# Returning the routed rows by indirect DMA through DRAM instead of by selection matrices on TensorE

## The chip, the core and the metric

One core of a Trainium2 chip runs the whole kernel in one launch. The metric is the device time of one execution in microseconds (us); the median of three runs of the kernel before is 292.20 us (292.16 to 292.22).

## What is computed

One transformer layer for x of 2 batches x 512 rows x 256 columns, float32: attention with 16 heads of width 128 over one shared latent k, a layernorm, then a network that only half of the rows pass (the 256 of 512 with the highest router score), and a second layernorm over all rows.

```python
x = _layernorm(x + attention(x, W_lat, b_lat, W_d, b_d, W_proj, b_proj))
scores = jnp.einsum('bsd,d->bs', x, router_weight) + router_bias[0]
top_scores, indices = jax.lax.top_k(scores, K)              # K = 256 of 512
weights = jax.nn.sigmoid(top_scores)
selected = jnp.take_along_axis(x, indices[:, :, None], axis=1)
h = jax.nn.gelu(jnp.einsum('bkd,df->bkf', selected, w1) + b1)      # 256 -> 1024
processed = jnp.einsum('bkf,fd->bkd', h, w2) + b2                  # 1024 -> 256
out = flat.at[flat_idx].add((processed * weights[:, :, None]).reshape(b * K, d))
x = _layernorm(out.reshape(b, s, d))
```

A row that isn't picked keeps its value, and its second layernorm depends on nothing but itself.

## The kernel before

Rows lie on 128 partitions: 4 tiles (TILES) per batch, `x1[:, b * 4 + j, :]` being 128 rows of 256. Every float32 product is three matmuls on two float32r words, high and low (`product`, L364 to L369): ScalarE writes a high word (`..._hi`), VectorE or POOL subtracts it to get the low one (`..._lo`).

The engines' programs are written by hand, each in order, with semaphores between them. Attention runs in periods, one per head and batch: units 0 to 31, and in period p TensorE does scores(p), turn(p-1), queries(p+1), project(p-2), values(p-1). `periods` (L262) walks through them; 3 to 12 are a loop, the rest is written out. Batch 0 ends its attention in period 17, so its layernorm, router, ranks and choice are put in pieces into periods 18 to 29 (names AT_OUT to AT_SELECT_T2, L278 to L280), on VectorE through `middle_piece` (L952) and `last_piece` (L980). On POOL each period splits W_d, W_proj and, in 13 to 28, a part of the network's weights.

The routing: `router_dots` (L1055) takes the dot with the router's weights on rows not yet normalised; `router_scores` scales them by the inverse deviation, which POOL computes as a power (`inverse_deviation`, L1290). TensorE turns the scores to a row (`turn_scores`, L521), `compare` (L1074) counts who beats whom, `rank_cols` (L527) sums on TensorE, and `ranks` (L1096) gives each row's rank. From the rank, `select` (L1104) builds a 0/1 matrix `sel` (a row's rank against 0 to 255), and TensorE gathers the picked rows, turned, into PSUM by 16 matmuls (`gather`, L545). ScalarE and VectorE take `xs_hi` and `xs_lo` from it. `rank_rows` (L536) turns the ranks to a row and `select_turned` (L1111) builds the opposite matrix `selT`.

The network: `hidden` (L563) makes 8 chunks of 6 matmuls, ScalarE the gelu and high word, POOL (batch 0) or VectorE (batch 1) the low word; `net_out` (L591) makes 24 matmuls for each of two groups of 128 picked rows; `start_net` (L580) puts b2 into PSUM beforehand. `net_high` (L817) and `net_low` (L1127) split the result, `scatter` (L602) spreads it over the 512 rows by 16 matmuls with `selT`, `add_up` (L1132) adds it to x1 times the weight and sums, and layernorm and stores follow (STORES, L354, from SP). For batch 1 the last variance goes through ScalarE's Square (L838), `last_variance` (L1179), POOL's power (L1320) and `last_apply` (L1185).

The order after attention: batch 0's gather stands in period 32 (two halves around the turns), hidden(0, 0..1) in period 33 ahead of the last projection; then TensorE runs hidden(0), start_net, net_out(0) with turn_scores(1) and rank_cols(1) between, rank_rows(1), gather(1), scatter(0), hidden(1), net_out(1), scatter(1). VectorE and ScalarE keep the matching order; VectorE does batch 0's add_up between the low words of hidden(1).

Of the kernel before, what the change touches and what calls it, by code (L numbers as in the profile page):

```python
# [28 lines left out]
F32 = mybir.dt.float32  # L29
F32R = mybir.dt.float32r  # L30
BF16 = mybir.dt.bfloat16
# [3 lines left out]
P = 128  # L35
# [21 lines left out]
def mk_layer_kernel(nc, x, W_lat, b_lat, W_d, b_d, W_proj, b_proj, router_w, router_b,  # L57
                    w1, b1, w2, b2, out):
    with ExitStack() as top:
# [7 lines left out]
        x1 = sb("x1", [P, BATCH * TILES, DIM])  # L67
# [14 lines left out]
        iota_col = sb("iota_col", [P, RCH])  # L82
# [13 lines left out]
        st = sb("st", [P, BATCH * 2, TILES, 6])  # L96
        mv = sb("mv", [P, BATCH * 2, TILES, 2])
        ve = sb("ve", [P, BATCH * 2, TILES])
        rstd = sb("rstd", [P, BATCH * 2, TILES])

        z_sum, minus_mean, squares = (sb(n, [P, TILES]) for n in ("z_sum", "minus_mean", "squares"))
# [8 lines left out]
        rank_row = sb("rank_row", [P, SEQ])  # L110
        rank = sb("rank", [P, TILES], F32R)
        half_tanh = sb("half_tanh", [P, BATCH, TILES])
        ones_row = sb("ones_row", [1, P], F32R)
        b2_hi, b2_lo = sb("b2_hi", [1, DIM], F32R), sb("b2_lo", [1, DIM], F32R)
        weight = sb("weight", [P, BATCH, TILES])
        x1_hi = sb("x1_hi", [P, BATCH * TILES, DIM], F32R)
        x1_lo = sb("x1_lo", [P, BATCH * TILES, DIM], F32R)
        sel = sb("sel", [P, BATCH * TILES, KEEP], F32R)
        selT = sb("selT", [P, BATCH, RCH, SEQ], F32R)
# [8 lines left out]
        def sems(name):  # L128
# [7 lines left out]
        b2_hi_done, b2_split = sem("b2_hi_done"), sem("b2_split")  # L136
# [25 lines left out]
        compared, rank_row_ready, rank_ready, rank_row_done, rank_done = (  # L162
            sems(n) for n in ("compared", "rank_row_ready", "rank_ready", "rank_row_done", "rank_done"))
        sel_done, selT_done, tanh_done, weight_done = (
            sems(n) for n in ("sel_done", "selT_done", "tanh_done", "weight_done"))
        x1_hi_done, x1_split = sems("x1_hi_done"), sems("x1_split")
# [3 lines left out]
        net_ready, net_hi_done, net_split = (  # L170
            sems(n) for n in ("net_ready", "net_hi_done", "net_split"))
        minus_mean_done, squares_done, last_var_done = (
            sem(n) for n in ("minus_mean_done", "squares_done", "last_var_done"))
        scattered, sum_done, stored = sems("scattered"), sems("sum_done"), sems("stored")
# [45 lines left out]
        net_hi = sb("net_hi", [P, BATCH, RCH, DIM], F32R)  # L220
        net_lo = sb("net_lo", [P, BATCH, RCH, DIM], F32R)
# [40 lines left out]
        def periods(eng, body):  # L262
# [11 lines left out]
        CONSTS = 7  # L274
# [5 lines left out]
         AT_SELECT, AT_SELECT_T, AT_SELECT_T2) = range(AT_OUT + 1, AT_OUT + 13)  # L280
# [7 lines left out]
        hidden_banks = [ps_s10, ps_s3, ps_s2, ps_y]  # L288

        def hidden_bank(f):  # L290
            return hidden_banks[f % len(hidden_banks)][:, 0:KEEP]

        def net_bank(b, r):
            return ps_out[:, 2 * r + b, :]

        def scatter_bank(b, j):


            if b:
                return (ps_t0, ps_t1, ps_s2, ps_s3)[j][:, 0:DIM]  # L300
            return (ps_t0, ps_t1)[j // 2][:, (j % 2) * DIM:(j % 2 + 1) * DIM]

        def chosen_bank(c):
            return (ps_s3, ps_s2)[c][:, 0:KEEP]

# [6 lines left out]
        def _(sp):  # L312
# [39 lines left out]

            periods(sp, period)
            STORES = [(0, 0, 2), (0, 2, 4), (1, 0, 2), (1, 2, 3), (1, 3, 4)]  # L354
            for b, j0, j1 in STORES:
                sp.wait_ge(ln_done[b], TILES + j1)
                sp.dma_start(out[b, j0 * P:j1 * P].rearrange("(j p) d -> p j d", p=P),
                             x1[:, b * TILES + j0:b * TILES + j1, :]).then_inc(stored[b], 16)
            for b in range(BATCH):
                sp.wait_ge(stored[b], 16 * len([st for st in STORES if st[0] == b]))  # L360

        @block.tensor
        def _(pe):
# [86 lines left out]
            def turn(at, n):  # L450
# [7 lines left out]
                if n == 1 and at.fixed - 1 in (AT_TURN, AT_SELECT, AT_RANK):  # L458

                    pe.wait_ge({AT_TURN: score_row_done, AT_SELECT: rank_row_done, AT_RANK: rank_done}[at.fixed - 1][0], 1)  # L460
# [75 lines left out]
            def rank_rows(b, dst):  # L536

                pe.wait_ge(rank_done[b], 1)
                for j in range(TILES):
                    last = pe.transpose(dst[:, j * P:(j + 1) * P].bitcast(F32R), rank[:, j:j + 1].to_broadcast([P, P]),  # L540
                                        ident_r[:, :])
                last.then_inc(rank_row_ready[b], 1)


            def gather(b, tiles=range(TILES)):  # L545

                pe.wait_ge(x1_split[b], 2)
                pe.wait_ge(negmax_done, 4 * UNITS)
                if b:
                    pe.wait_ge(xs_split[0], CH)  # L550
                    pe.wait_ge(gelu_done[0], FCH)
                for j in tiles:
                    pe.wait_ge(sel_done[b], j + 1)
                    for c in range(CH):
                        t, cs = b * TILES + j, slice(c * P, (c + 1) * P)
# [790 lines left out]
```

## Time and profile before

| | us |
|---|---|
| median of three runs | 292.20 |
| the profiled execution | 292.16 |
| its span in the trace | 290.40 |

| engine | busy us | share of the span |
|---|---|---|
| TensorE (PE) | 280.5 | 97% |
| VectorE (DVE) | 224.0 | 77% |
| ScalarE (ACT) | 211.4 | 73% |
| POOL | 144.9 | 50% |

The span is the time from the first to the last recorded event of the core; 1.76 us of the execution lie outside it. A busy share is an average over the whole kernel: what bounds a stretch has to be read from that stretch. In the traces L12 is line 12 of the kernel, and start times count from the span's start. The next instruction of an engine may start before the end of the one before it, since matmuls and others are pipelined: of a group of n, the time from start to start counts. No DMA of this kernel is issued from POOL.

### The profile page before, as it was taken

What the parts mean: (1) busy time and instruction counts of PE and PEld (TensorE: products, weight loads), DVE (VectorE), ACT (ScalarE), POOL (GpSimd) and SP (SyncE); (2) the same over time, 40 slices, a digit from 0 to 9 for tenths busy, and PEclk for the clock granted to TensorE, in tenths of its full rate; (3) what the DMA queues carried; (4) which work ended last, traced back from release to release, by engine and by line L of the source; (5) the groups of instructions that cost most, each with busy time, mean ns of one, the idle gap of its engine ahead of it and who ended that gap; (6) DMA issues with size and microseconds to landing.
All of it is one profiled execution on the core that took longest, in us unless ns stands there. A gap on an engine that the chain in (4) does not pass through costs nothing.

```text
span 290.4 us, 6306 instructions
## 1 busy us (share of the span) xinstructions
PE 280.5 (97%) x1942; PEld 255.1 (88%) x1942; DVE 224.0 (77%) x699; ACT 211.4 (73%) x582; POOL 144.9 (50%) x204
## 2 busy tenths in 40 slices
PE   6998999999999999999999999999999999999991
PEld 3777999999999999999999999999999999999991
DVE  2688777777777777777888788999888877498685
ACT  3588777777777777777777777777798777663632
POOL 3647643444343448655556756656557612184013
PEclk9999999999999999999999999999999999999997
DMA  6583111111111111111101111111110000000004
GB/s 190 119 283 98 39 38 36 36 36 36 36 36 36 36 37 38 36 35 40 34 26 42 32 35 36 40 36 36 40 37 20 19 21 0 2 1 0 2 9 136
DMA packets 17738, 13.42 MB, mean 46 GB/s; under 512 B 1433, under 2 KB 17458, under 8 KB 17714
## 3 DMA queue, kind: packets, MB, share of 16 engines
q1 hardware_dynamic: 17714, 13.13, 15.4%
q8 instruction: 12, 0.20, 0.3%
q14 instruction: 12, 0.10, 0.1%
HBM read 12.07 MB, written 1.05 MB: 45 GB/s over the span
## 4 chain that ended last, share of the span: by engine, by line
PE 88%; DVE 6%; ACT 2%; issue 1%; SPq 1%; DMA 1%; POOL 1%; POOLq 0%; DVEq 0%; ACTq 0%
PE bank L367 18%; PE bank L369 17%; PE bank L368 17%; PE bank L468 8%; PE ps_out L367 7%; PE ps_out L369 6%; PE ps_out L368 6%; PE bank L518 2%; PE bank L446 2%; DMA bias_rows<-in_L_ffn_b 1%; DVE x L1052 1%; PE bank L556 1%; DVE sel L1060 1%; PE bank L558 1%; DVE beats L1087 1%
## 5 line engine op out<-in xcount | busy, mean ns | idle before, releaser
L725 ACT ACTIVATE probs<-probs,negmax 128x512 f32<-128x512 f32 (+3 forms) x128 | 72.6, 574 | 7.1 <-DVE negmax L891 5.7
L1213 POOL TENSOR_TENSOR wd_hi<-wd_raw,zero 128x256 fp32r<-128x256 f32 x32 | 24.7, 772 | 89.4 <-DVE probs L948 83.8
L732 ACT CAST pT_hi<-bank 128x512 fp32r<-128x512 f32 (+2 forms) x96 | 43.5, 488 | 28.7 <-PE bank L468 28.7
L891 DVE CUSTOM_DVE_ANT_0 probs<-bank,mask_row 128x512 f32<-128x512 f32 (+3 forms) x128 | 59.2, 482 | 0.6 <-PE bank L369 0.6
L898 DVE TENSOR_TENSOR pT_lo<-bank,pT_hi 128x512 fp32r<-128x512 f32 (+2 forms) x96 | 53.0, 553 | 6.2 <-ACT pT_hi L732 5.9
L468 PEld LDWEIGHTS bank<-ident_r,prob_words 128*128 128x128 f32 x320 | 34.4, 141 | 5.3 <-issue 0.2
L367 PE MATMUL ps_out<-wp_hi,yT_hi 128*128 128x256 f32 x128 | 38.4, 300 | 0.1
L367 PE MATMUL bank<-kT_hi,qT_hi 128*128 128x512 f32 (+2 forms) x96 | 37.3, 389 | 0.2 <-DVE qT_lo L845 0.2
L908 DVE TENSOR_TENSOR yT_lo<-bank,yT_hi 128x512 fp32r<-128x512 f32 x32 | 22.1, 691 | 18.5 <-PE bank L369 13.3
L369 PE MATMUL ps_out<-wp_hi,yT_lo 128*128 128x256 f32 x128 | 36.2, 283 | 0.0
L368 PE MATMUL ps_out<-wp_lo,yT_hi 128*128 128x256 f32 x128 | 36.1, 282 | 0.0
L468 PE MATMUL bank<-ident_r,prob_words 128*128 128x128 f32 x320 | 35.0, 240 | 0.0
L367 PE MATMUL bank<-pT_hi,k_hi 128*128 128x512 f32 (+2 forms) x96 | 32.9, 342 | 0.9 <-DVE pT_lo L898 0.9
L369 PE MATMUL bank<-kT_hi,qT_lo 128*128 128x512 f32 (+2 forms) x96 | 32.6, 340 | 0.0
L368 PE MATMUL bank<-pT_lo,k_hi 128*128 128x512 f32 (+2 forms) x96 | 32.4, 337 | 0.0
L368 PE MATMUL bank<-kT_lo,qT_hi 128*128 128x512 f32 (+2 forms) x96 | 32.3, 337 | 0.0
L369 PE MATMUL bank<-pT_hi,k_lo 128*128 128x512 f32 (+2 forms) x96 | 32.2, 335 | 0.0
L1213 POOL TENSOR_TENSOR wp_hi<-wp_raw,zero 128x256 fp32r<-128x256 f32 x32 | 23.6, 738 | 13.7 <-DVE probs L948 13.7
L948 DVE TENSOR_SCALAR probs<-probs,rinv 128x384 f32<-128x384 f32 (+2 forms) x96 | 28.3, 351 | 1.1
L764 ACT ACTIVATE probs<-probs,rinv 128x512 f32<-128x512 f32 x32 | 23.2, 724 | 8.2 <-DVE rinv L942 8.2
L845 DVE SCALAR_TENSOR_TENSOR qT_lo<-bank,bias_cols,qT_hi 128x384 fp32r<-128x384 f32 x32 | 19.7, 616 | 12.1 <-ACT qT_hi L695 11.7
L367 PE MATMUL bank<-xT_hi,wd_hi 128*128 128x512 f32 x64 | 27.8, 434 | 0.0
(150 smaller groups left out, 744.0 us busy)
## 6 DMA issues: line engine op xcount, KB each, us to landing
wd_raw<-in_L_attn_W_d SPq DMA_DIRECT2D x32, 128.0 KB, 2.2
wp_raw<-in_L_attn_W_proj SPq DMA_DIRECT2D x32, 128.0 KB, 2.1
wf_raw<-in_L_ffn_w SPq DMA_DIRECT2D x2, 1024.0 KB, 6.5
x_nat<-in_L_attn_x SPq DMA_DIRECT2D x4, 256.0 KB, 3.0
out<-x SPq DMA_DIRECT2D x3, 256.0 KB, 2.2
out<-x SPq DMA_DIRECT2D x2, 128.0 KB, 2.0
wlat_raw<-in_L_attn_W_lat SPq DMA_DIRECT2D x1, 128.0 KB, 3.5
bproj_all<-in_L_attn_b_proj SPq DMA_DIRECT2D x1, 128.0 KB, 3.7
```

The lines of the kernel that those rows point to most:

```text
L367: pe.matmul(dst, lh, rh, start=first, stop=False, skip_group_check=check)
L368: pe.matmul(dst, lh, rl, start=False, stop=False, skip_group_check=check)
L369: return pe.matmul(dst, ll, rh, start=False, stop=last, skip_group_check=check)
L468: last = pe.transpose(dst[:, a:a + P].bitcast(F32R), prob_words[s][:, P_OFF[j] + i * P:P_OFF[j] + (i + 1) * P], ident_r[:, :])
L725: act.activation(p_tile(s, j), p_tile(s, j), ACT.Exp, bias=negmax[:, s, j:j + 1], scale=-1.0, accum_out=sums[:, s, j:j + 1]).then_inc(exp_ ...
L732: act.copy(pT_hi[:, turns[n][3]], turns[n][2]).then_inc(pt_hi_done, 1)
L764: act.mul(p_tile(at.place(0), 3), p_tile(at.place(0), 3), rinv[:, at.place(0), 3:4]).then_inc(norm_act, 1)
L891: dve.tensor_tensor_reduce(p_tile(s, j), score_bank[j], mask_row[:, (TILES - 1 - j) * P:], -SCALE, -MASKED, ALU.add, ALU.min, accum_out=ne ...
L898: dve.tensor_tensor(pT_lo[:, dst], src, pT_hi[:, dst].bitcast(F32), ALU.subtract).then_inc(pt_lo_done, 1)
L908: dve.tensor_tensor(yT_lo[:, :], ps_y[:, :], yT_hi[:, :].bitcast(F32), ALU.subtract).then_inc(y_lo_done, 1)
L948: dve.tensor_scalar(p_tile(s, j), p_tile(s, j), rinv[:, s, j:j + 1], None, ALU.mult).then_inc(norm_dve, 1)
L1213: pool.tensor_tensor(hi, src, nothing, ALU.add).then_inc(hi_done, 1)
```

## The change

Picked rows no longer go through selection matrices, but for batch 1's gather.

Batch 0: each row of x1 gets two words more, its gate (sigmoid of the score) and its number. After the ranks POOL issues four indirect DMAs (`push`), each writing 128 rows to DRAM at their rank (`ranked`); SP loads the first 256 back (`picked`, `load_picked`, period 29); TensorE turns them by four transposes (`turn_picked`, period 31) into the xs of the network. Batch 1 keeps `sel` and `gather`, is pushed and loaded too, but only for what follows.

All 512 rows of a batch are normalised without a network's share into `z_all` and stored. The network's output of a batch (`net_bank`) is added to `z`, which POOL begins as b2 times gate plus picked row (`begin_z`); two tiles of `z` are normalised and `put_back` writes them by two indirect DMAs per batch onto the stored output. So `selT`, `rank_rows`, `start_net`, `net_high`, `net_low` and both scatters are gone. hidden(0) starts a period earlier, with chunks 0 to 2 in period 32 and 3 and 4 in 33, and its banks are three.

```diff
+            def load_picked(b):
+                sp.wait_ge(pushed[b], 16 * TILES)
+                sp.dma_start(picked[:, b].bitcast(F32), ranked[b][0:KEEP, :].rearrange("(r p) d -> p r d", p=P)
+                             ).then_inc(picked_in[b], 16)
...
+                if at.fixed == AT_REST_2:
+                    load_picked(0)
...
+            store_all(0)
+            load_picked(1)
+            store_all(1)
...
+            def turn_picked():
+                pe.wait_ge(picked_in[0], 16)
+                pe.wait_ge(negmax_done, (UNITS - 1) * 4 + 1)
+                for c in range(CH):
+                    for r in range(RCH):
+                        last = pe.transpose(ps_s3[:, c * KEEP + r * P:c * KEEP + (r + 1) * P].bitcast(F32R),
+                                            picked[:, 0, r, c * P:(c + 1) * P], ident_r[:, :])
+                last.then_inc(gathered[0], 1)
...
-            hidden(0, range(2, 6))
-            start_net()
-            hidden(0, range(6, FCH))
-            net_out(0, 0, range(0, 4))
+            hidden(0, range(5, FCH))
+            net_out(0, 0)
             turn_scores(1, ps_t0)
-            net_out(0, 0, range(4, FCH))
-            net_out(0, 1, range(0, 4))
+            net_out(0, 1, range(0, 6))
             rank_cols(1, ps_t1)
-            net_out(0, 1, range(4, FCH))
-            rank_rows(1, ps_t0)
-            gather(1)
-            scatter(0)
+            net_out(0, 1, range(6, FCH))
+            gather()
             hidden(1, range(FCH))
             for r in range(RCH):
                 net_out(1, r)
-            scatter(1)
```

VectorE after the periods (routing of batch 1, low words, the two tails):

```diff
-            layernorm_apply(1, 0, range(TILES))
+            layernorm_apply(1, 0, (0, 1))
             compare(1, range(TILES))
             losses(1)
-            net_low(0, 0)
+            layernorm_apply(1, 0, (2, 3))
             ranks(1, ps_t1)
-            select(1, range(TILES))
-            net_low(0, 1)
-            chosen_low(1)
-            for q in range(RCH):
-                select_turned(1, q)
-            weights(1)
+            select((0, 1))
+            dve.wait_ge(x1_hi_done, 2)
+            dve.tensor_tensor(x1_lo[:, 2:TILES, :], x1[:, TILES + 2:2 * TILES, :], x1_hi[:, 2:TILES, :].bitcast(F32),
+                              ALU.subtract).then_inc(x1_split[1], 1)
+            select((2, 3))
+            rank_numbers()
+            gates(1)
+            chosen_low()
...
+            for f in range(FCH):
+                hidden_low(f)
+                if f < TILES:
+                    layernorm_stats(1, 1, (f,))
+                    aggregate(1, 1, (f,))
+                elif f == TILES:
+                    variance(1, 1, 0)
+                    variance(1, 1, 1)
+                else:
+                    layernorm_apply(1, 1, (f - TILES - 1,))
+            layernorm_apply(1, 1, (3,))
+            for r in range(RCH):
+                add_up(0, r)
+            layernorm_stats(0, 2, range(RCH))
+            aggregate(0, 2, range(RCH))
+            variance(0, 2, 0)
+            add_up(1, 0)
+            layernorm_apply(0, 2, range(RCH))
...
+            last_variance(0)
             last_apply(0)
-            last_variance((3,))
-            for j in range(1, TILES):
-                last_apply(j)
+            add_up(1, 1)
+            last_variance(1)
+            last_apply(1)
```

POOL:

```diff
+            def push(b):
+                pool.wait_ge((rank_no_done if b else rank_done)[b], 1)
+                pool.wait_ge(gate_done[b], 1)
+                pool.wait_ge(consts, CONSTS)
+                for j in range(TILES):
+                    pool.wait_ge(ln_done[b], j + 1)
+                    pool.indirect_dma_start(ranked[b], bass.IndirectOffsetOnAxis(ap=rank_no[:, b, j:j + 1], axis=0),
+                                            x1_row[:, b * TILES + j, :], None).then_inc(pushed[b], 16)
+
+            def begin_z(b):
+                pool.wait_ge(picked_in[b], 16)
+                pool.wait_ge(rows_in, 64)
+                for r in range(RCH):
+                    pool.tensor_scalar(z[:, b, r, :], b2_all[:, :], gate(b, r), None, ALU.mult).then_inc(b2_gated[b], 1)
+                    pool.wait_ge(b2_gated[b], r + 1)
+                    pool.tensor_tensor(z[:, b, r, :], z[:, b, r, :], picked_words(b, r, 0, DIM),
+                                       ALU.add).then_inc(z_begun[b], 1)
+
+            def put_back(b, r):
+                pool.wait_ge(stored[b], 32)
+                pool.wait_ge(ln_done[b], 2 * TILES + r + 1)
+                pool.indirect_dma_start(out.rearrange("b s d -> (b s) d"),
+                                        bass.IndirectOffsetOnAxis(ap=picked[:, b, r, ROW_NO:ROW_NO + 1].bitcast(U32), axis=0),
+                                        z[:, b, r, :], None).then_inc(routed[b], 16)
...
             for f in range(FCH):
-                if f in (2, 3):
-                    inverse_deviation(1, 0, f - 2)
+                if f in (6, 7):
+                    inverse_deviation(1, 0, f - 6)
                 hidden_low(f)
+            x1_low(0)
+            push(1)
             for half in range(2):
-                x1_low(1, half)
-            for half in range(2):
-                inverse_deviation(0, 1, half)
...
+                inverse_deviation(1, 1, half)
+            begin_z(1)
+            inverse_deviation(0, 2, 0)
+            for r in range(RCH):
+                put_back(0, r)
+            for r in range(RCH):
+                pool.wait_ge(last_var_done, r + 1)
+                pool.tensor_tensor(rstd[:, 2 * BATCH + 1, r:r + 1], ve[:, 2 * BATCH + 1, r:r + 1],
+                                   minus_half[:, r:r + 1], ALU.pow).then_inc(rstd_done[1], 1)
+                put_back(1, r)
```

push(0) stands at the end of POOL's period 27 (AT_PUSH). `layernorm_stats(b, 1, ...)`, `aggregate`, `variance` and `layernorm_apply(b, 1, ...)` now serve the rows without a network's share, those with 2 the picked ones; batch 0's stand in periods 27 to 31.

## Rows read from the trace of the kernel before

**Rows 1.** Stretches of all engines: us, busy (x instructions) of PE, PEld, DVE, ACT, POOL; clock; DMA

```profile
171.12:178.47 7.35, 7.35 (x54) 6.74 (x52) 6.48 (x23) 5.73 (x17) 4.54 (x6) 1.00 0.13 36
208.63:216.32 7.69, 7.69 (x60) 7.08 (x58) 6.16 (x21) 5.90 (x17) 4.40 (x6) 1.00 0.12 35
254.07:264.79 10.72, 10.32 (x80) 9.53 (x80) 10.48 (x35) 6.18 (x16) 8.62 (x11) 1.00 0.00 1
264.79:270.72 5.93, 5.93 (x58) 5.93 (x59) 4.17 (x13) 1.53 (x4) 0.67 (x1) 1.00 0.01 3
270.72:276.47 5.75, 5.75 (x50) 5.75 (x49) 3.43 (x15) 4.59 (x13) 0.00 (x0) 1.00 0.00 0
276.47:282.33 5.86, 5.86 (x52) 5.86 (x51) 4.75 (x19) 1.65 (x5) 1.38 (x2) 1.00 0.00 0
282.33:290.40 8.07, 2.12 (x17) 1.74 (x15) 4.52 (x19) 2.44 (x9) 2.19 (x4) 0.81 0.39 130
```

**Rows 2.** The chain that ended last, from 235 us: start us, us, what

```profile
253.39 0.70 DVE x L1014
...
262.85 1.90 DVE beats L1087 x8
...
285.34 1.71 POOL rstd L1320 x3
...
287.57 0.41 DVE x L1188
```

**Rows 3.** TensorE's groups from 238 us: count | busy us, mean ns | idle

```profile
L556 PE MATMUL bank<-sel,x_hi 128*128 128x256 f32 x16 | 4.2, 297 | 0.0
L617 PE MATMUL bank<-net_hi,selT 128*128 128x256 f32 x16 | 4.0, 287 | 0.0
```

**Rows 4.** POOL in order of time

```profile
216.68 1.29 POOL L1300 TENSOR_TENSOR x_lo<-x,x_hi 128x512 fp32r<-128x512 f32 x1 [3.41 <-ACT x_hi L775]
...
257.29 0.80 POOL L1295 TENSOR_TENSOR rstd<-ve,minus_half 128x2 f32<-128x2 f32 x1 [0.17 <-DVE ve L1042]
258.06 3.99 POOL L1306 TENSOR_TENSOR hid_lo<-hid,hid_hi 128x256 fp32r<-128x256 f32 x5
...
279.46 0.69 POOL L1295 TENSOR_TENSOR rstd<-ve,minus_half 128x2 f32<-128x2 f32 x1 [14.00 <-DVE ve L1039]
```

**Rows 5.** VectorE in order of time: start us, us, line, operation [idle before]

```profile
259.27 0.57 DVE L1068 TENSOR_TENSOR dots_scaled<-dots,rstd 128x4 f32<-128x4 f32 x1
...
260.53 2.32 DVE L1052 TENSOR_SCALAR x<-x,mv,rstd 128x256 f32<-128x256 f32 x4
...
264.77 0.70 DVE L1094 TENSOR_TENSOR lost<-behind,won 128x4 f32<-128x4 f32 x1
...
265.91 1.14 DVE L1108 TENSOR_SCALAR sel<-iota_row,rank 128x256 fp32r<-128x256 f32 x4
...
273.15 0.43 DVE L1168 TENSOR_TENSOR hid_lo<-hid,hid_hi 128x256 fp32r<-128x256 f32 x1 [2.32 <-ACT hid_hi L799]
...
278.15 0.74 DVE L1026 BATCH_NORM_STATS2 st<-x 128x6 f32<-128x256 f32 x2
...
281.26 1.39 DVE L1052 TENSOR_SCALAR x<-x,mv,rstd 128x256 f32<-128x256 f32 x4 [0.54 <-POOL rstd L1295]
...
283.89 0.48 DVE L1139 SCALAR_TENSOR_TENSOR x<-bank,weight,x 128x256 f32<-128x256 f32 x1 [0.69 <-PE bank L618]
```

**Rows 6.** ScalarE in order of time

```profile
268.79 0.67 ACT L815 ACTIVATE xs_hi<-bank 128x256 fp32r<-128x256 f32 x2 [1.16 <-PE bank L558]
...
284.42 0.51 ACT L838 ACTIVATE squared<-x,z_sum 128x256 f32<-128x256 f32 x1 [1.68 <-DVE x L1139]
```

**Rows 7.** SP's stores (L357): issue in ns, min/median/max, and landing

```profile
L357 SPq DMA_DIRECT2D out<-x x5: 373/394/402, 282.0 to 288.0; - x5
...
DMA to landing us min/median/max: 1.9/2.2/2.3
```

**Rows 8.** POOL's groups over the whole span: the longest operation

```profile
L1286 POOL TENSOR_TENSOR x<-x_nat,bproj_all 128x1024 f32<-128x1024 f32 x2 | 4.8, 2389 | 0.0
```

More of the change, by code:

```diff
@@ L628, in period @@
                 if at.fixed == UNITS:
-                    gather(0, range(0, 2))
+                    hidden(0, range(0, 2))
                 if at.live(-1):
@@ L644, in period @@
                 else:
+                    if at.fixed == AT_PICKED:
+                        turn_picked()
                     if at.fixed == UNITS:
-                        gather(0, range(2, TILES))
+                        hidden(0, range(2, 3))
                     if at.fixed == UNITS + 1:
-                        hidden(0, range(0, 2))
+                        hidden(0, range(3, 5))
                     if at.live(-2):
@@ L972, in middle_piece @@
                     layernorm_apply(0, 0, (2,))
-                if at.fixed == AT_SELECT:
-                    select(0, (0,))
-                if at.fixed == AT_SELECT_T:
-                    select(0, (3,))
-                if at.fixed == AT_SELECT_T2:
-                    select_turned(0, 1)
+                if at.fixed == AT_PUSH:
+                    layernorm_stats(0, 1, (0,))
+                if at.fixed == AT_REST:
+                    layernorm_stats(0, 1, (2,))
+                if at.fixed == AT_REST_2:
+                    aggregate(0, 1, range(TILES))
+                    variance(0, 1, 0)
+                    variance(0, 1, 1)
+                if at.fixed == AT_REST_3:
+                    layernorm_apply(0, 1, (0,))
             def last_piece(at):
@@ L1111, in select_turned, with select @@
-            def select_turned(b, q):
-                dve.wait_ge(rank_row_done[b], 1)
-                dve.tensor_scalar(selT[:, b, q, :], rank_row[:, :], iota_col[:, q:q + 1], None,
-                                  ALU.is_equal).then_inc(selT_done[b], 1)
-            def weights(b):
+                dst = rank[:, :] if b else rank_no[:, 0, :]
+                dve.tensor_tensor(dst, src[:, 0:TILES], lost[:, b, :], ALU.add).then_inc(rank_done[b], 1)
+            def select(tiles):
+                dve.wait_ge(rank_done[1], 1)
+                for j in tiles:
+                    dve.tensor_scalar(sel[:, j, :], iota_row[:, :], rank[:, j:j + 1], None,
+                                      ALU.is_equal).then_inc(sel_done, 1)
@@ L1169, in _ @@
                                   ALU.subtract).then_inc(hid_split[1], 1)
+            for f in range(FCH):
+                hidden_low(f)
                 if f < TILES:
-                    add_up(0, f)
-            for half in range(2):
-                layernorm_stats(0, 1, (2 * half, 2 * half + 1))
-                aggregate(0, 1, (2 * half, 2 * half + 1))
-                variance(0, 1, half)
-            net_low(1, 0)
-            layernorm_apply(0, 1, range(TILES))
-            net_low(1, 1)
@@ L1277, in period @@
                         inverse_deviation(0, 0, half)
-                if at.fixed in (AT_SELECT, AT_SELECT_T):
-                    x1_low(0, at.fixed - AT_SELECT)
+                if at.fixed == AT_PUSH:
+                    push(0)
+                if at.fixed == AT_REST_3:
+                    for half in range(2):
+                        inverse_deviation(0, 1, half)
+                if at.fixed == AT_PICKED:
+                    begin_z(0)
             def start_x1(b):
```

367 lines of the change are left out of this document (154 added, 213 removed).

## Prediction

> **What bounds the kernel now.** I read four views in this order: the stretches of the last 40 us, the chain that ended last, each engine's order of time in that stretch, and the DMA issues. The stretches [rows 1] show TensorE busy without a gap in an attention period (7.35 of 7.35 us) and again from 264.79 to 282.33. Between them, 254.07 to 264.79, VectorE is busy 10.48 of 10.72 us while TensorE fills in with batch 0's network: there the chain runs through VectorE, from the last projection's sum at 253.39 to the comparisons that end at 264.75 [rows 2]. From 282.33 to the end it is a relay: last scatter, sums, variance, the power on POOL (1.71 us for three), the last normalisation, a store [rows 2]. So three things set the end: VectorE's routing chain of batch 1, then TensorE from the gather on, then the relay.
>
> The profiled run took 292.16 us with a span of 290.40, so 1.76 us lie outside the span; the median of the runs is 292.20. I sum against the span.
>
> **Part 1, inside attention.** Period 27 (with the four rank transposes and the wait for their row) is 7.69 us against 7.35 [rows 1]: removing them gives back 0.34. `turn_picked` puts four transposes into period 31, at 0.06 to 0.12 us each (+0.3); behind them ScalarE takes xs_hi in one pass of 512 and VectorE its low word, ahead of `turned(2)`, and TensorE's `values` waits for that (+0.3). The batch 0 gather goes (its 16 matmuls are half of the gathers', of which [rows 3] has the x1_hi half), but the same place takes three more hidden chunks (18 matmuls) ahead of the last projection. 48 matmuls take 5.75 us [rows 1], so one is 0.12: -1.9 and +2.2. Net: the last projection ends at 254.1 as before, bounds -0.6 and +0.8.
>
> The four pushes of batch 0 stand on POOL behind the splits of period 27. Queued behind them are the next weight splits, which are needed a whole period later; before, the low word of x1 (1.29 us [rows 4]) stood in the same place and TensorE lost nothing by it. Pushes of up to about 7 us together are hidden, so I cost them at nothing; SP's wait for them holds up only the loads of W_proj, a period early. The norm of all rows of batch 0 (stats, variance, apply) takes the place of select and select_turned on VectorE, about as many microseconds: nothing.
>
> **Part 2, routing of batch 1.** The chain on VectorE keeps its shape but only two of the four applications stand before the comparison. Before, the applications start at 260.53 and the four take 2.32 us beside a working POOL, 1.39 us alone [rows 5]. After:
> start 260.8 (the two powers on POOL now stand behind six and seven low words of 0.80 us each [rows 4], so the second ends near 259.6 where it ended at 258.1, and VectorE wants it at 259.27 [rows 4, 5]: +0.3); two applications 0.7, 261.5; wait for the turned scores 0.1; compare 1.90 [rows 2], 263.5; loss, between 0.2 and the 0.70 of [rows 5], 0.3, 263.8; two applications 0.7, 264.5; rank 0.15; two selects 0.57 (half of 1.14 [rows 5]), 265.2; low word of x1, now on VectorE, 0.70 (the size of the sum in [rows 2]), 265.9; two selects 0.57, 266.5; last matmuls of the gather 0.7, 267.2; xs_hi 0.35 (half of 0.67 [rows 6]) and its low word 0.45, 268.0.
> So hidden(1) starts at 268.0, not at 270.72: **-2.7 us**. The scatter of batch 0 (16 matmuls, half of L617's 16 [rows 3] and their partners with net_lo: 1.9 us) and the second set of rank transposes no longer stand on TensorE, and the scatter no longer covers the wait for xs. TensorE has 66 network matmuls (7.9 us) and 0.8 us of turns to put into 13 us, so it is not the bound here. Bounds for this part -3.3 and -1.8.
>
> **Part 3, the network of batch 1.** 5.75 + 5.86 us [rows 1] as before, to 279.6. VectorE's first low word comes 2.43 us after hidden(1) starts (273.15 [rows 5] against 270.72), so at 270.45. Then it does a low word (0.34), stats (0.37) and an aggregate per chunk, 0.92 us, where ScalarE delivers one each 0.72: 274.15 after four; low word and two variances, 274.8. The applications of batch 1 wait for powers (0.69 [rows 4], 275.6) with the last low words queued behind them on VectorE, and TensorE's net_out waits for those: +0.7, so TensorE ends near 280.3 against 282.33. Net of parts 1 to 3: **-2.0 us**.
>
> **Part 4, the relay.** Before, it took 8.07 us [rows 1]. After, there is no scatter(1), no net_hi and net_lo, and only two tiles of sums. But POOL now issues four indirect stores, and it issues put_back(0,0) and put_back(0,1) ahead of batch 1's first power; VectorE has last_apply(0), which waits for that power, ahead of add_up(1,1); so the two stores of batch 0 stand on the path. The unknown is D, the time POOL is held by one indirect DMA of 128 rows. The trace of before has none. Nearest rows: SP's issue of a store, 0.39 us [rows 7], as the low end; POOL's passes of 0.69 (a power) and 1.29 us (512 elements) [rows 4]; its pass over 1024 elements, 2.39 us [rows 8], as the high end. I take D = 1.0, between the two short POOL rows, since 128 addresses are work in software like theirs. Landing after it: 2.2 less 0.4 from issue [rows 7], 1.8, of which some runs beside the generation: 1.6.
> Applications and low words after 275.6: 2.1 us, with 0.5 for POOL's `begin_z(1)` beside them ([rows 5]: 2.32 against 1.39), 278.2; two add_ups 0.8 [rows 5], stats 0.74, aggregate 0.3, variance 0.2, 280.2; power 0.77, 281.0; apply, 281.4; put_back twice, 0.1 + 0.3 (the second application held off by POOL) + 2D, 283.8; power 0.7, 284.5; last_apply(0), 284.9; add_up(1,1) 0.48, 285.35; Square 0.51 and its read-out 0.2 [rows 6], 286.1; variance 0.2, 286.3; power 0.77, 287.05; apply 0.45, 287.5; put_back(1,1) 0.1 + D, 288.6; landing 1.6, 290.2; 0.1 to the end of the span. **Span 290.3, run 292.1.** What the network gains (-2.0) the relay gives back (+1.9). Each 0.1 us of D is worth 0.3 us.
>
> What the profile shows of POOL and VectorE together is that they hold each other up: the same four applications, 2.32 against 1.39 us [rows 5]. The Trainium skill (SBUF — State Buffer, "SBUF: two separate sides", the box on DVE blocking DMA) says the same lock stops POOL from writing descriptors while VectorE runs such an operation, and has a POOL-issued DMA at about 620 ns alone. By 0.62 for D the sum would be 291.0; the row has the lock for computing operations, and no row has it for descriptors.
>
> **Rivals.**
> B, the stores are cheap: D near 0.5, like SP's issue. Then 3 x 0.5 us less and the second application hardly held: span 288.6, **run 290.4**. For it: 128 rows are little data, and SP needs 0.39 [rows 7]. Against it: POOL takes 0.69 us even for an operation on two elements per lane [rows 4]. The Trainium skill (DMA: Bandwidth & Descriptors, "Anatomy of one DMA") calls the generation small and puts the 2 us into completion, which speaks for B; no run shown here has a DMA from POOL.
> C, POOL becomes the bound: D above 1.25. Then put_back(1,0) too delays the last power, and pushes and `load_picked(1)` (4D and two landings after 266.8) reach into `begin_z(1)`. At D = 1.8: +2.4, +0.55 (put_back(1,0)), +0.35 (held application), +0.5 (begin_z late): span 294.1, **run 295.9**. It decides from D = 1.25 on; slower by the measurable starts at 292.8.
> D, the early half fails: batch 0's picked rows come late to period 31, or TensorE's clock falls. It waits some 4 us in pieces between 254 and 268, where before it waited 0.4; the clock granted is 1.00 in all stretches but the last, where it is 0.81 with TensorE mostly idle [rows 1]. A clock halved for hidden(1) would add some 3 us or more: **run 297**.
>
> **How the numbers follow.** Forecast A (D from 0.8 to 1.25, run 291.2 to 293.1): 0.38. B 0.27, C 0.30, D 0.05. The likeliest case gives 292.1, its own range 291.2 to 293.1. A measurement of this kernel tells 0.2%, 0.6 us, from no change. Faster (below 291.6): B and 0.11 of A, 0.38. Same: 0.20. Slower: 0.07 of A, C and D, 0.42. The range runs from B with somewhat less contention, 289.6, to C at D = 1.8, 296.0.
>
> **What would show it.** Part 1: batch 0's period 31 longer by 0.3 to 0.6 us and the last projection ending at 253.5 to 254.9. Part 2: hidden(1) starting near 268.0. Part 3: net_out(1,1) ending near 280.3, with a wait on hid_lo of batch 1. Part 4: the power of batch 1's first tile right behind put_back(0,1), add_up(1,1) waiting behind last_apply(0) for over 3 us, and from the end of TensorE to the end of the span about 10 us. Wrong if POOL is idle before the last powers, or if the relay follows TensorE directly.

## The result and the profile after

The changed kernel takes 295.03 us (median of four runs, 294.94 to 295.28) against 292.19 us of the kernel before beside it: ratio 1.0098, 95% interval 1.0083 to 1.0113, so 1.0% slower. The profiled execution took 294.99 us with a span of 293.3; 1.7 us lie outside. I had forecast 292.1 us; the range of 289.6 to 296.0 holds the time, the likeliest case (291.2 to 293.1) doesn't. Of the three directions I had given slower the largest chance, 0.42, but the sum itself stood at no change.

The stretches of the kernel after, with the columns of [rows 1]:

```profile
core 0: us, PE busy (x) PEld busy (x) DVE busy (x) ACT busy (x) POOL busy (x), PEclk, DMA share, GB/s
208.72:216.06 7.34, 7.34 (x57) 6.73 (x54) 5.91 (x20) 5.56 (x16) 6.29 (x8) 1.00 0.18 55
238.09:244.90 6.81, 6.64 (x52) 6.02 (x50) 5.60 (x18) 5.20 (x16) 4.77 (x6) 1.00 0.13 41
254.60:268.30 13.70, 11.61 (x97) 10.56 (x96) 11.87 (x44) 4.49 (x12) 7.17 (x9) 1.00 0.00 0
268.30:275.20 6.90, 6.90 (x58) 6.90 (x59) 4.06 (x16) 4.78 (x14) 3.01 (x4) 1.00 0.26 82
275.20:281.23 6.03, 5.13 (x40) 4.68 (x39) 5.35 (x20) 0.97 (x3) 5.13 (x7) 1.00 0.39 127
281.23:293.30 12.07, 0.15 (x2) 0.00 (x0) 2.30 (x10) 1.20 (x4) 5.70 (x7) 0.63 0.13 43
```

The period of 7.69 us of [rows 1] is 7.34. The network of batch 1 starts at 268.30 instead of 270.72 (2.42 earlier), TensorE's last matmul for the network ends at 281.39 instead of 282.33 (0.94 earlier), and from there to the end of the span it is 11.9 us instead of 8.07 (the last stretch above begins 0.16 before that matmul's end). In these 12 us TensorE, VectorE and ScalarE are nearly idle; POOL is busy 5.70. What it does there, POOL in order of time (start us, us, line, operation, idle before and what ended it):

```profile
280.94 0.72 POOL L1276 TENSOR_TENSOR rstd<-ve,minus_half 128x2 f32<-128x2 f32 x1 [0.52 <-DVE ve L1020]
282.95 1.07 POOL L1310 DMA_INDIRECT out<-z,picked  x1 [1.29 <-DVE z L1034]
284.32 0.96 POOL L1310 DMA_INDIRECT out<-z,picked  x1 [0.30 <-issue]
285.31 0.58 POOL L1335 TENSOR_TENSOR rstd<-ve,minus_half 128x1 f32<-128x1 f32 x1
287.13 1.04 POOL L1310 DMA_INDIRECT out<-z,picked  x1 [1.24 <-DVE z L1175]
288.19 0.58 POOL L1335 TENSOR_TENSOR rstd<-ve,minus_half 128x1 f32<-128x1 f32 x1
290.01 1.04 POOL L1310 DMA_INDIRECT out<-z,picked  x1 [1.24 <-DVE z L1175]
```

And VectorE beside it, which waits for those powers and has `add_up(1,1)` behind the first of them:

```profile
281.70 0.74 DVE L1034 TENSOR_SCALAR z<-z,mv,rstd 128x256 f32<-128x256 f32 x2 [0.50 <-POOL rstd L1276]
...
285.92 0.41 DVE L1175 TENSOR_SCALAR z<-z,minus_mean,rstd 128x256 f32<-128x256 f32 x1 [3.36 <-POOL rstd L1335]
286.25 0.48 DVE L1112 SCALAR_TENSOR_TENSOR z<-bank,picked,z 128x256 f32<-128x256 f32 x1
...
287.40 0.15 DVE L1166 TENSOR_SCALAR ve<-squares 128x1 f32<-128x1 f32 x1 [0.67 <-ACT squared L805]
...
288.81 0.41 DVE L1175 TENSOR_SCALAR z<-z,minus_mean,rstd 128x256 f32<-128x256 f32 x1 [1.19 <-POOL rstd L1335]
```

Two things are to be read here. A passing power holds POOL for 0.58 us and an indirect store for 0.96 to 1.07 us, one beside the other in one queue: the power at 285.31 starts when the second store ends. And a store whose data has just come starts late: VectorE's pass of 285.92 ends at 286.33, the store starts at 287.13, 0.80 later (0.79 for the last one, 0.83 for the first), while one that was already released starts 0.30 behind the store before it. The powers have no such delay: the variance of 287.40 is there at 287.55 and only the store keeps POOL until 288.17; at 280.94 the power starts 0.14 behind its variance (280.63 and 0.17).

The last store starts at 290.01 and the span ends at 293.3, 3.3 us on. It lands 2.5 us after its start, at 292.5, which is 1.4 us behind the end of POOL's hold (291.05) and 0.8 us before the end of the span. The chain's last pieces, and the row on the landing of the four stores, counted from each one's start:

```profile
286.39 0.74 issue
287.13 1.04 POOL out L1310
...
289.27 0.50 issue
289.78 1.27 POOLq L60
```

```profile
DMA to landing us min/median/max: 2.4/2.5/2.5
```

### The profile page after: what moved, and what is told of

The parts are those of the page before. It is cut to its first block, busy times and chain, and to the rows that moved or that the text cites. A ratio compares the mean times of both kernels' runs of the same rounds, so it can differ in the third digit from the quotient of the medians.

```text
span 293.3 us, 6209 instructions
## 1 busy us (share of the span) xinstructions
PE 274.9 (94%) x1886; PEld 248.8 (85%) x1886; DVE 221.8 (76%) x698; ACT 206.9 (71%) x569; POOL 159.0 (54%) x219
## 3 DMA queue, kind: packets, MB, share of 16 engines
HBM read 12.60 MB, written 2.63 MB: 52 GB/s over the span
## 4 chain that ended last, share of the span: by engine, by line
PE 82%; DVE 6%; POOL 3%; ACT 3%; issue 2%; SPq 1%; DMA 1%; POOLq 0%; DVEq 0%; ACTq 0%
PE bank L384 18%; PE bank L386 17%; PE bank L385 17%; PE bank L485 8%; PE ps_out L384 6%; PE ps_out L386 5%; PE ps_out L385 5%; PE bank L535 2%; PE bank L463 2%; POOL out L1310 1%; POOL hid_lo L1317 1%; POOL rstd L1276 1%; DMA bias_rows<-in_L_ffn_b 1%; DVE beats L1069 1%; DVE z_all L1034 1%
## 5 line engine op out<-in xcount | busy, mean ns | idle before, releaser
L812 DVE SCALAR_TENSOR_TENSOR qT_lo<-bank,bias_cols,qT_hi 128x384 fp32r<-128x384 f32 x32 | 19.7, 617 | 11.9 <-ACT qT_hi L679 11.3
```

## The experiments

Theory R says that the relay after TensorE sets the time, with POOL's queue in it, where stores stand ahead of the powers. Theory T says that the time follows TensorE's end. Each ratio is to the kernel before, measured beside that run (292.07 to 292.15). Up to `hidden(1)` all runs but 6 have the changed kernel's program, yet their traces reach it at 268.2 to 268.9 (268.30 in the changed kernel): a few tenths between the same point of two traces say nothing by themselves.

**1. The powers ahead.** POOL issues batch 1's first power ahead of both stores of batch 0, and its second ahead of both stores of batch 1. VectorE is untouched.

```diff
+            last_power(0)
             for r in range(RCH):
                 put_back(0, r)
+            last_power(1)
             for r in range(RCH):
-                pool.wait_ge(last_var_done, r + 1)
-                pool.tensor_tensor(rstd[:, 2 * BATCH + 1, r:r + 1], ve[:, 2 * BATCH + 1, r:r + 1],
-                                   minus_half[:, r:r + 1], ALU.pow).then_inc(rstd_done[1], 1)
                 put_back(1, r)
```

> The changed kernel, with POOL's first power of batch 1 ahead of the two indirect stores of batch 0; nothing else moves. Theory R (the relay behind POOL's indirect stores sets the end): the power runs at 282.5 instead of 285.3, add_up(1,1) at 283.5 instead of 286.25, and the last indirect store starts near 287.9 instead of 290.0: 292.9 us, 2.1 less than the changed kernel's 295.0. Theory T (the network and the late first half set the end; the stores only fill a wait): no change, 294.8 to 295.2.

Measured: 292.87 us (292.67 to 293.19), 2.2 us under the changed kernel; ratio to before 1.0021 (0.9999 to 1.0042). Its POOL:

```profile
282.46 0.55 POOL L1333 TENSOR_TENSOR rstd<-ve,minus_half 128x1 f32<-128x1 f32 x1 [0.91 <-DVE ve L1166]
283.23 1.18 POOL L1310 DMA_INDIRECT out<-z,picked  x1 [0.22 <-issue]
284.71 0.96 POOL L1310 DMA_INDIRECT out<-z,picked  x1 [0.30 <-issue]
285.70 0.57 POOL L1333 TENSOR_TENSOR rstd<-ve,minus_half 128x1 f32<-128x1 f32 x1
286.46 1.17 POOL L1310 DMA_INDIRECT out<-z,picked  x1 [0.19 <-issue]
287.94 0.96 POOL L1310 DMA_INDIRECT out<-z,picked  x1 [0.30 <-issue]
```

No store starts 0.8 us late any more, since all data is there before: gaps of 0.19 to 0.30. The last one starts at 287.94, not 290.01. Theory R's number was met without any work being taken away. The expectation names the first power alone; the edit also moves the second one ahead of `put_back(1,0)`, so the 2.2 us belong to both moves together. What is left of POOL's stores on the path is two pairs, one ahead of the last power.

**2. Plain stores.** SP stores `z` to fixed rows by plain DMAs in place of POOL's indirect stores. The output's picked rows thus stand in the wrong places: it leaves out the return to the rows' own places.

```diff
+                for r in range(RCH):
+                    sp.wait_ge(ln_done[b], 2 * TILES + r + 1)
+                    sp.dma_start(out[b, r * P:(r + 1) * P, :], z[:, b, r, :]).then_inc(routed[b], 16)
...
-            for r in range(RCH):
-                put_back(0, r)
...
-                put_back(1, r)
```

> The changed kernel, with the four indirect stores of z replaced by four plain stores from SP onto fixed rows, so the picked rows land in the wrong places (that part of the computation is left out). Theory R: POOL has only powers left in the relay, and a store costs 0.4 to issue and 2.1 to land: the last store starts near 286.1, the run ends at 290.1 us, 4.9 less. Theory T: at most 1.5 less (the last store's own landing): 293.5 or more.

Measured: 289.76 us, ratio 0.9926 (0.9901 to 0.995), where theory R had 290.1 and theory T 293.5 or more. TensorE ends as in the changed kernel (last matmul 281.21 against 281.11); the span is 288.2. POOL's last power now waits for VectorE's variance, not for a store:

```profile
284.97 0.56 POOL L1337 TENSOR_TENSOR rstd<-ve,minus_half 128x1 f32<-128x1 f32 x1 [1.75 <-DVE ve L1170]
```

So the indirect stores, with the powers that stood behind them, are worth 5.3 us at the tail in this order of the queues, more than the loss to before; without them the kernel is 2.3 us faster than the one before.

**3. TensorE earlier.** VectorE does all low words of batch 1 before its four applications, so TensorE's output matmuls don't wait for them.

```diff
-                else:
-                    layernorm_apply(1, 1, (f - TILES - 1,))
-            layernorm_apply(1, 1, (3,))
+            layernorm_apply(1, 1, range(TILES))
```

> The changed kernel, with VectorE's eight low words of hidden(1) ahead of all four applications of the norm of batch 1. Theory R: TensorE no longer waits (0.69 and 0.20 us) and ends 0.9 to 1.1 us earlier, near 280.3, but the relay starts from VectorE's variance of batch 0's picked rows and POOL, which stay where they are: 294.7 to 295.1 us. Theory T: the time follows TensorE's end: 294.0 us.

Measured: 295.52 us (294.86 to 295.62), 0.4 above theory R's range and far from theory T's 294.0. The last matmul starts at 280.23 instead of 281.11, 0.9 earlier, and the last store at 290.63 instead of 290.01. Theory T falls: VectorE's applications, not TensorE, lead into the relay.

```profile
277.21 2.33 DVE L1034 TENSOR_SCALAR z_all<-x_row,mv,rstd 128x256 f32<-128x256 f32 x4 [0.25 <-POOL rstd L1274]
...
281.26 0.17 DVE L1020 TENSOR_SCALAR ve<-mv 128x2 f32<-128x2 f32 x1
```

The four applications run beside POOL's `begin_z(1)` and take 2.33 us, the figure of [rows 5] beside a working POOL; batch 0's variance is 0.6 later than in the changed kernel (280.63), of which 0.26 is this trace's later start of `hidden(1)` (268.56).

**4. Two stores more.** Behind batch 0's stores POOL issues two more of the same size to a spare tensor in DRAM.

```diff
             for r in range(RCH):
                 put_back(0, r)
+            for r in range(RCH):
+                put_spare(r)
```

> The changed kernel, with two more indirect stores of 128 rows on POOL (batch 0's picked rows again, to a spare tensor in DRAM) right behind batch 0's two. Theory R: each holds POOL for 0.96 and 0.30 us before the next, all of it on the path: +2.5 us, 297.5. Theory T: hidden, +0.3 at most, 295.3.

Measured: 297.51 us (297.2 to 297.65), 2.48 more than the changed kernel; theory R had 297.5.

```profile
284.36 0.96 POOL L1317 DMA_INDIRECT out<-z,picked  x1 [0.30 <-issue]
285.62 0.96 POOL L1308 DMA_INDIRECT spare<-z,picked  x1 [0.30 <-issue]
286.88 0.96 POOL L1308 DMA_INDIRECT spare<-z,picked  x1 [0.30 <-issue]
287.86 0.58 POOL L1344 TENSOR_TENSOR rstd<-ve,minus_half 128x1 f32<-128x1 f32 x1
```

Each costs 0.96 and a gap of 0.30, 1.26 us, and all of it comes out at the end. The stores of batch 0 are on the path, and their price is that of POOL's hold, not of the DMA's landing.

**5. Batch 0 early.** VectorE does batch 0's sums right behind `chosen_low`, where it waits 2.3 us in the changed kernel; POOL returns batch 0 behind the pushes; VectorE begins batch 1's `z`; the low words stand ahead of the applications as in run 3, and `add_up(1,1)` ahead of `last_variance(0)`; both last powers go ahead of batch 1's stores.

```diff
+            for r in range(RCH):
+                add_up(0, r)
+            layernorm_stats(0, 2, range(RCH))
+            aggregate(0, 2, range(RCH))
+            variance(0, 2, 0)
+
             for f in range(FCH):
                 hidden_low(f)
...
+                if f == TILES - 1:
+                    layernorm_apply(0, 2, range(RCH))
...
+            inverse_deviation(0, 2, 0)
+            for r in range(RCH):
+                put_back(0, r)
             for half in range(2):
                 inverse_deviation(1, 1, half)
-            begin_z(1)
+            for r in range(RCH):
+                last_power(r)
```

> The changed kernel with the relay taken apart: VectorE sums batch 0's picked rows in the gap before hidden(1)'s first low word, POOL puts them back right behind the pushes (from about 274 on), VectorE takes over begin_z(1) in two passes, the low words of hidden(1) stand ahead of the applications, both last powers stand ahead of batch 1's two indirect stores. Theory R (only what POOL and its stores put behind TensorE's end costs; the first half of the change does gain): TensorE ends near 280.1, the last indirect store starts near 283.9, 3.3 us before the end of the span: 288.9 us, 6 less than the changed kernel and 3.2 less than the kernel before. Theory L (POOL's whole load, pushes and all, is the bound wherever it stands): the pushes to 272.2 and then 2.4 + 2.2 us of powers and stores of batch 0 push the norm and the stores of all rows of batch 1 late; 291.5 or more.

Measured: 290.98 us (290.59 to 291.23), ratio 0.9957 (0.9943 to 0.997): faster than both kernels, but 2 us short of what I expected. POOL and VectorE of this kernel:

```profile
275.84 1.88 POOL L1314 DMA_INDIRECT out<-z,picked  x1 [2.53 <-DVE z L1034]
278.02 0.96 POOL L1314 DMA_INDIRECT out<-z,picked  x1 [0.30 <-issue]
279.00 1.38 POOL L1280 TENSOR_TENSOR rstd<-ve,minus_half 128x2 f32<-128x2 f32 x2
...
286.32 0.96 POOL L1314 DMA_INDIRECT out<-z,picked  x1 [0.30 <-issue]
```

```profile
275.71 1.09 DVE L1142 TENSOR_TENSOR hid_lo<-hid,hid_hi 128x256 fp32r<-128x256 f32 x3
...
280.42 1.38 DVE L1034 TENSOR_SCALAR z_all<-x_row,mv,rstd 128x256 f32<-128x256 f32 x4 [2.63 <-POOL rstd L1280]
281.72 0.47 DVE L1112 SCALAR_TENSOR_TENSOR z<-bank,picked,z 128x256 f32<-128x256 f32 x1
```

I had made the fault of the change over again one place earlier: the two powers of batch 1's norm stand behind two stores, one of which takes 1.88 us; VectorE waits 2.63 us for them, and `add_up(1,0)`, whose data is ready, stands behind the applications that wait.

**6. A chunk later.** As 5, with one hidden chunk fewer ahead of the last projection (chunk 2 moves one period on, chunk 4 behind the projection), and POOL's powers of the scores one chunk earlier.

```diff
-                    if at.fixed == UNITS:
-                        hidden(0, range(2, 3))
...
-                        hidden(0, range(3, 5))
+                        hidden(0, range(2, 4))
...
-            hidden(0, range(5, FCH))
+            hidden(0, range(4, FCH))
...
-                if f in (6, 7):
-                    inverse_deviation(1, 0, f - 6)
+                if f in (5, 6):
+                    inverse_deviation(1, 0, f - 5)
```

> As the one before, and one of the five hidden chunks that stand ahead of the last projection moves behind it (and POOL's two powers of batch 1's first layernorm one low word earlier). Theory: the 0.5 us by which the last projection came later than before was TensorE's own work ahead of it (18 matmuls in, 16 out, four transposes, waits); a chunk is 0.72 us, so the last projection ends 0.7 us earlier, TensorE has idle time behind it to take the chunk, and the run gets 0.5 to 0.7 us shorter: 288.3 us. Rival: POOL's low words of hidden(0), not the projection, set the router's scores; then no gain, 288.9 us.

Measured: 291.33 us (291.17 to 291.87), 0.35 more than 5, where I expected less. From the start of period 31 to the last projection's sum it is 15.5 us instead of 15.8, so only 0.3 of the expected 0.7 came, and the second power comes no more than that sooner:

```profile
259.06 0.88 POOL L1278 TENSOR_TENSOR rstd<-ve,minus_half 128x2 f32<-128x2 f32 x1
```

In the kernel of 5 it starts at 259.33. What it gains there, 0.27, is lost twice over: POOL still has two low words to do, beside which `score` takes 0.67 us (0.23 in 5), and VectorE waits 0.47 us for the turned scores (0.22 in 5). `hidden(1)` starts at 269.05 (268.62 in 5). So the rival's "no gain" holds, and the 0.5 us that Part 1 costs did not come back by moving matmuls.

**7. Beginning z on POOL again.** As 5, but POOL does `begin_z(1)` as in the changed kernel.

```diff
-            dve.wait_ge(picked_in[1], 16)
-            for r in range(RCH):
-                dve.scalar_tensor_tensor(z[:, 1, r, :], b2_all[:, :], gate(1, r), picked_words(1, r, 0, DIM),
-                                         ALU.mult, ALU.add).then_inc(z_begun[1], 1)
...
             for half in range(2):
                 inverse_deviation(1, 1, half)
+            begin_z(1)
```

> As e5_early_back, but begin_z(1) stays on POOL (two multiplications and two additions, 3.4 us, behind the powers of all rows' norm). It prices POOL's place ahead of the last powers. Theory R: begin_z(1) ends near 281.1, add_up(1,1) and both powers follow, the last store starts near 284.5: 289.5 us, 0.6 more than e5_early_back. Theory L: 2 us or more above it.

Measured: 292.27 us, ratio 1.0011 (0.9997 to 1.0026), 1.3 more than 5. The four passes of `begin_z(1)` run from 280.08 to 283.48, behind the stores and the powers, and the last store starts at 287.43 instead of 286.32:

```profile
282.84 0.64 POOL L1302 TENSOR_TENSOR z<-z,picked 128x256 f32<-128x256 f32 x1
284.15 0.58 POOL L1329 TENSOR_TENSOR rstd<-ve,minus_half 128x1 f32<-128x1 f32 x1 [0.67 <-DVE ve L1166]
```

The 1.3 us lie between the 0.6 of theory R and the 2 of theory L, so neither was met. `begin_z` is on the path again: the first of batch 1's powers follows it by 0.67 us, at 284.15 where it stands at 283.11 in 5.

**8. Powers ahead of all stores.** As 5, with three places changed: POOL's powers of batch 1's norm ahead of batch 0's stores, their variances earlier on VectorE, and `last_variance(0)` ahead of `add_up(1,1)`.

```diff
+                if f in (1, 3):
+                    variance(1, 1, f // 2)
...
-            add_up(1, 1)
             last_variance(0)
+            add_up(1, 1)
             last_apply(0)
...
             inverse_deviation(0, 2, 0)
-            for r in range(RCH):
-                put_back(0, r)
             for half in range(2):
                 inverse_deviation(1, 1, half)
+            for r in range(RCH):
+                put_back(0, r)
```

> The reordered kernel of the run before (batch 0's norm early, 290.98 us) with three queue positions changed. POOL: both powers of batch 1's all-row norm ahead of put_back(0,*), with VectorE writing their variances right behind the statistics of chunks 1 and 3. VectorE: last_variance(0) ahead of add_up(1,1). Nothing is added or removed. Theory Q (the 2 us that the earlier version missed were two in-order queues: POOL's two stores of 1.88 and 0.96 us ahead of the norm's powers, and VectorE's add_up(1,*) behind the applications that waited 2.63 us for those powers): the powers end near 275.4, put_back(0,0) starts near 275.6 (POOL busy before it, so 0.2 us behind it, not 0.8) and put_back(0,1) ends near 278; VectorE's four applications start at 277.8 instead of 280.42; add_up(1,0) at 279.2, add_up(1,1) right behind TensorE's end at 280.5; the last powers near 280.6 and 281.9; put_back(1,0) near 282.8, put_back(1,1) near 284.1 instead of 286.32; span 287.2, run 288.9 (bounds 288.3 to 289.6). Rival S (the end is set by the stores of all rows landing before put_back(1,*), or by the DMA queue, not by the order of the queues): put_back(1,*) waits for the landing of the stores whatever the order, the last one starts at 285 or later, and the run stays at 290 or above.

Measured: 289.05 us (288.79 to 289.54), ratio to before 0.9896 (0.988 to 0.9913): 1.0% faster than the kernel before and 2% faster than the changed one. The three changes were made together, so the 1.9 us against 5 are not divided among them. POOL, then VectorE:

```profile
276.61 1.75 POOL L1313 DMA_INDIRECT out<-z,picked  x1 [0.29 <-issue]
278.66 1.05 POOL L1313 DMA_INDIRECT out<-z,picked  x1 [0.30 <-issue]
280.83 0.58 POOL L1332 TENSOR_TENSOR rstd<-ve,minus_half 128x1 f32<-128x1 f32 x1 [1.12 <-DVE ve L1169]
282.55 0.55 POOL L1332 TENSOR_TENSOR rstd<-ve,minus_half 128x1 f32<-128x1 f32 x1 [1.15 <-DVE ve L1169]
283.29 1.04 POOL L1313 DMA_INDIRECT out<-z,picked  x1 [0.18 <-issue]
284.64 0.96 POOL L1313 DMA_INDIRECT out<-z,picked  x1 [0.30 <-issue]
```

```profile
278.14 1.38 DVE L1034 TENSOR_SCALAR z_all<-x_row,mv,rstd 128x256 f32<-128x256 f32 x4
...
281.16 0.48 DVE L1112 SCALAR_TENSOR_TENSOR z<-bank,picked,z 128x256 f32<-128x256 f32 x1 [0.42 <-PE bank L386]
```

VectorE's applications start at 278.14 (280.42 in 5) and the last store at 284.64 (286.32). Theory Q's time was 288.9; theory S falls, the landing of the other stores doesn't hold the last ones. TensorE's end (its last matmul starts at 280.77) leads into the relay here: `add_up(1,1)` waits 0.42 us for it, and the second power waits 1.15 us for the variance behind that.

## Why the prediction was wrong

**Part 1: the terms nearly right, their sum not drawn.** The terms were -0.34, +0.3, +0.3, -1.9 and +2.2, which is +0.56, and I wrote "as before". The sum of the last projection starts at 253.90 instead of 253.39 [rows 2]: **+0.5**. At the start of period 31 the changed kernel is 0.40 us ahead (238.09 against 238.49), near the -0.34 of the sum, but not by it alone, and so by luck: period 27 gave back 0.35, and period 25 took the same 0.35 (7.68 us for 7.33), because VectorE writes batch 0's gates there, an operation of 0.69 us that no term had; the rest are gains of 0.1 to 0.2 in other periods, which I had not forecast either. Period 31 takes 6.74 us instead of 6.02: 0.38 for the four transposes, 0.34 for TensorE's wait behind VectorE's work on the picked rows, together +0.72 for the +0.6 of the sum. The exchange of 16 matmuls for 18 costs 0.18, where I had 0.3.

```profile
244.23 0.39 PE L384 MATMUL bank<-pT_hi,k_hi 128*128 128x256 f32 x1 [0.17 <-DVE pT_lo L865]
```

The pushes of batch 0 cost nothing, as said; four of them stand 1.26 us apart in front of a weight split that is needed much later, and TensorE is busy 7.34 of 7.34 us:

```profile
217.93 0.96 POOL L1292 DMA_INDIRECT ranked<-x_row,rank_no  x1 [0.30 <-issue]
218.91 0.75 POOL L1192 TENSOR_TENSOR wd_hi<-wd_raw,zero 128x256 fp32r<-128x256 f32 x1
```

**Part 2: right.** `hidden(1)` starts at 268.30, forecast 268.0. With 0.5 us more at its start the chain itself was 0.2 better than summed.

**Part 3: the wait too small.** TensorE ends at 281.39 against 280.3: 0.3 from the start, the rest waits for batch 1's low words, as named but with about 1.5 us rather than 0.7 (281.39 - 268.30 = 13.09 us, against 11.61 without a wait; from start to start 0.96 and 0.47 us where 0.12 is usual, and some after):

```profile
277.07 0.39 PE L384 MATMUL bank<-wf_hi,hid_hi 128*128 128x256 f32 x1 [0.69 <-DVE hid_lo L1142]
...
277.89 0.39 PE L384 MATMUL bank<-wf_hi,hid_hi 128*128 128x256 f32 x1 [0.20 <-DVE hid_lo L1142]
```

In this kernel the term is worth nothing: the chain of Part 4 starts from VectorE's applications, and in run 3 TensorE ended 0.9 earlier and the time was no shorter. Of the 2 us that Parts 1 to 3 were to bring, 0.94 came.

**Part 4: this step failed, and not by D.** The mechanism is the one described: the first power right behind `put_back(0,1)`, `add_up(1,1)` behind `last_apply(0)` (a wait of 3.36 us), TensorE long idle. D was set at 1.0, and the trace has 0.96 to 1.07. But the relay takes 11.9 us where the sum had 10.0, so it gives back 3.8 instead of 1.9, and the span ends at 293.3, not at 290.3. The 3.0 us, point by point along the sum:

| step of the sum | forecast | measured | adds |
|---|---|---|---|
| variance of batch 0 | 280.2 | 280.8 | +0.6 |
| its first tile normalised | 281.4 | 282.1 | +0.1 |
| end of put_back(0,1) | 283.8 | 285.3 | +0.8 |
| variance of batch 1's second tile | 286.3 | 287.5 | -0.3 |
| its power | 287.05 | 288.8 | +0.5 |
| last store off POOL | 288.6 | 291.05 | +0.7 |
| end of the span | 290.3 | 293.3 | +0.6 |

Three terms of it were mis-sized. First, between a release and a store that had been waiting for it I put 0.1 us; it is 0.79 to 0.83, twice on the path, +1.4. In run 1, with the data there beforehand, the same stores start 0.19 to 0.30 us after what stands before them; its 2.2 us hold this term and the powers' waits together, so no run has the term alone, and what makes the 0.8 stays open. Second, I let `put_back(1,0)` hold up the last power only from D = 1.25 on. As that store starts 0.8 late, it lies on the power's time already at D = 1.0: the variance is there at 287.55, the power starts at 288.19 instead of 287.69, +0.5. Third, what follows the last landing: from the end of POOL's hold to the end of the span it is 2.25 us, not 1.7. The landing itself came as summed (1.4 us behind the hold, I had 1.6); but behind it stand 0.8 us, not 0.1. The kernel before had 0.5 there already: its last store, issued at 288.0, lands 1.9 us later, at 289.9, and its span ends at 290.4. One term was right by luck: the 0.3 between the two stores. I had put it down to a second application held off by POOL; the two applications took 0.74 us and were done at 282.44, and the 0.30 is the gap that stands between any two of these stores. The first of the table's rows is Part 2's 0.3 and VectorE's wait for a low word (0.39 idle at 273.89) that I hadn't summed.

**Rivals.** The time is close to C's (295.9), the cause isn't quite: C had a hold D above 1.25, and the hold is 0.96 to 1.07; only with the gap of 0.30 does a store in a row cost 1.26. Of C, its point on `put_back(1,0)` came about. B's cheap store did not: 0.96 us and a 0.30 gap. By the Trainium skill (DMA: Bandwidth & Descriptors, "Anatomy of one DMA"), generation is small and about 2 us are completion; in the traces the landing comes 2.4 to 2.5 us after a store's start, 1.4 of them behind POOL's hold, and the hold of 0.96 us for 128 addresses is not small; by run 4 it is paid in full. VectorE's applications did not stop a store: in run 8 one that ran beside them (278.66, the applications 278.14 to 279.52) took 1.05 us. Rival D's lower clock did not happen: 1.00 in every stretch until 281.23, although TensorE is idle 2.1 of 13.70 us from 254.60 on.

**Where the expected gain went.** It is real: run 2 without the indirect stores is 2.3 us faster than before. Run 8 keeps them and gets 3.1, by the order of the queues and by beginning batch 1's `z` on VectorE. What the indirect stores still cost in the order of run 8 was not measured.

## What to carry to other kernels

An indirect store is work on POOL, not just a transfer: give each its place in POOL's queue (here 0.96 us and a gap of 0.30 for 128 rows), and put every small operation that another engine waits for ahead of it. A store that waits for its data starts later than one whose data is there; near the end, put the waiting inside other work, as run 1 does. When a sum shows that one store's delay reaches a next power "from D on", add all delays of that store, not D alone.

## What the runs showed of the hardware

- An indirect DMA of 128 rows of 1 KB holds POOL 0.96 to 1.07 us (up to 1.18 in run 1), the next starts 0.30 later; with late data the start is 0.8 us behind the release, where a power's is 0.14.
- Batch 0's first store took 1.88 us in runs 5 and 6, 1.89 in run 7 and 1.75 in run 8. Each time VectorE ran low words without a break beside it (three in 1.09 us in run 5, four in 1.42 in run 8), and each time the store ended 0.91 to 0.93 us behind the last of them, as if its hold began there. A single one of 0.4 us, as beside the pushes of the changed kernel, left them at 0.96. By the Trainium skill (SBUF — State Buffer, "SBUF: two separate sides") a VectorE instruction with two SBUF inputs, if it starts first, keeps the port pair that it shares with POOL for its whole length, against a POOL operation that reads SBUF; the rows fit, but no run moved the low words away with all else kept, so that cause is argued, not shown.
- VectorE's four applications, 1.39 us alone, took 2.33 beside POOL's passes (run 3), and 1.38 beside an indirect store (run 8, 278.14 to 279.52, the store 278.66 to 279.71): neither holds the other up by more than 0.1 us.
- From the last landing to the end of the span it is 0.8 to 0.9 us where the last store is POOL's, and 0.5 us where it is SP's (run 2 and the kernel before).
